# Flamingo gated block: tokens stationary in the first product, the product transposed on TensorE, and a new order within the step

## What is computed

```
def xattn(h, token_ids, W):
    expert = min(clip(token_ids, 0, 24999) // 6250, 3)
    g = silu(einsum('bsd,fd->bsf', h, W[e])); u = einsum('bsd,fd->bsf', h, W[e])
    y = einsum('bsf,df->bsd', g * u, W[e])            # taken where expert == e
def ffn(x, Wr, br, Wd, bd, Wu, bu):
    gates = softmax(x @ Wr + br + bonus); w = top 2 of 8, normalized
    h = relu(einsum('btd,edr->betr', x, Wd) + bd); eo = h @ Wu + bu
    return sum over e of w[e] * eo[e]
x = x + tanh(g_xattn) * xattn(layernorm(x), tokens, ctx)
x = x + tanh(g_ffn) * ffn(layernorm(x), ...)
```

## Time and profile before

| | before |
|---|---|
| median of three runs | 239.81 us (238.13 to 240.24) |
| the profiled execution | 238.26 us, span 236.5 us |
| mean granted TensorE clock | 0.938 |
| PE busy | 181.9 us, 77% of the span |
| VectorE busy | 140.0 us, 59% |
| ScalarE busy | 121.8 us, 51% |
| POOL busy | 115.6 us, 49% |
| the chain that ended last | POOL 28%, issue 26%, PE 15%, VectorE 14%, its queue 9% |

### The profile page before, as it was taken

The page is one execution under the profiler, slowest core; times in us unless marked ns, Lnnn a source line. Parts: engine busy times, 40 slices in busy tenths (PEclk is TensorE's granted clock), DMA queues, the critical chain, the costliest instruction groups (busy, mean ns, idle before and its releaser), DMA issues.

```text
span 236.5 us, 5853 instructions
## 1 busy us (share of the span) xinstructions
PE 181.9 (77%) x1558; PEld 119.6 (51%) x1559; DVE 140.0 (59%) x452; ACT 121.8 (51%) x254; POOL 115.6 (49%) x261
## 2 busy tenths in 40 slices
PE   1767978789999887888698787889869985835550
PEld 1746953546666555464455645556456562413310
DVE  5778837576766665757656565545755745444421
ACT  2875893983476645628365473654734535401200
POOL 3678443536155837455473534534446446422421
PEclk9999997999999999999999999999999999597655
DMA  5947751323139343331333313343134032120111
GB/s 178 355 110 259 160 124 39 94 47 84 55 87 136 78 99 98 88 91 44 89 85 95 89 44 91 70 110 89 44 89 99 34 89 49 41 81 8 44 44 44
DMA packets 43028, 21.62 MB, mean 91 GB/s; under 512 B 38632, under 2 KB 38760, under 8 KB 43008
## 3 DMA queue, kind: packets, MB, share of 16 engines
q1 hardware_dynamic: 40448, 12.99, 23.5%
q0 software_dynamic: 2560, 8.39, 11.1%
HBM read 9.06 MB, written 4.19 MB: 56 GB/s over the span
## 4 chain that ended last, share of the span: by engine, by line
POOL 28%; issue 26%; PE 15%; DVE 14%; DVEq 9%; ACT 4%; ACTq 2%; DMA 1%; POOLq 1%
POOL rs L501 6%; POOL xs L483 4%; DVEq L1229 4%; DVEq L1230 3%; POOL neg_mean L567 3%; POOL half_second L540 3%; PE ps_aT L682 3%; POOL mrs L502 3%; POOL ve L500 2%; DVE xs L1236 2%; POOL half_first L538 2%; ACT dev L870 2%; DVE w_rep L1289 2%; DVE w_lo L1096 2%; POOL hot_slot L476 2%
## 5 line engine op out<-in xcount | busy, mean ns | idle before, releaser
L682 PE MATMUL ps_aT<-hT,w_hi 128*128 128x128 f16 x304 | 64.8, 228 | 1.7 <-DVE prod L1212 1.0
L683 PE MATMUL ps_aT<-hT,w_hi 128*128 128x128 f16 x304 | 63.4, 223 | 0.0
L684 PE MATMUL ps_aT<-hT,w_lo 128*128 128x128 f16 x304 | 63.3, 223 | 0.0
L682 PEld LDWEIGHTS ps_aT<-hT,w_hi 128*128 x304 | 30.0, 99 | 15.1 <-issue 4.1
L658 PE MATMUL ps_y<-w_hi,pT_hi 128*128 x76 | 30.3, 399 | 2.4 <-DVE w_lo L1096 1.9
L1236 DVE SCALAR_TENSOR_TENSOR xs<-ps_y,y_t,xs 128x512 f32 x19 | 14.3, 751 | 30.2 <-issue 27.1
L683 PEld LDWEIGHTS ps_aT<-hT,w_hi 128*128 x304 | 30.5, 100 | 1.3
L660 PE MATMUL ps_y<-w_hi,pT_lo 128*128 x76 | 30.3, 399 | 0.0
L684 PEld LDWEIGHTS ps_aT<-hT,w_lo 128*128 x304 | 30.0, 99 | 0.6
L659 PE MATMUL ps_y<-w_lo,pT_hi 128*128 x76 | 30.2, 397 | 0.0
L870 ACT ACTIVATE dev<-xs,neg_mean 128x512 f32<-128x512 f32 (+1 forms) x15 | 10.8, 722 | 30.1 <-POOL neg_mean L567 30.1
(11 more groups left out here) (217 smaller groups left out, 424.8 us busy)
## 6 DMA issues: line engine op xcount, KB each, us to landing
w_nat<-in_ctx_dram SPq DMA_DIRECT2D x4, 1024.0 KB, 7.6
xs<-in_x_dram,rows_of POOLq DMA_INDIRECT x16, 3.6
wd_nat<-in_L_ffn_Wd_dram SPq DMA_DIRECT2D x4, 64.0 KB
wu_nat<-in_L_ffn_Wu_dram SPq DMA_DIRECT2D x1, 256.0 KB
hT<-h_parts SPq DMA_TRANSPOSE x16, 2.7
out_dram<-xs,rows_of POOLq DMA_INDIRECT x16, 2.9
h2T<-h_parts SPq DMA_TRANSPOSE x15, 2.8
b_in<-in_L_ffn_bd_dram SPq DMA_DIRECT2D x1, 64.0 KB
```

The costliest lines, as they stand in the source:

```text
L682: mm(ps_aT[:, n, :], hi, hT[:, q, kc, :], start=(kc == 0), stop=False)
L683: mm(ps_aT[:, n, :], hi, hT[:, q, KC + kc, :], start=False, stop=False)
L684: last = mm(ps_aT[:, n, :], lo, hT[:, q, kc, :], start=False, stop=(kc == KC - 1))
```

## The change

The first product has the tokens stationary (`split_product` into ps_a): 12 matmuls of 512 columns. Its result has tokens in partitions, so the silu and the product work on that layout, and TensorE transposes the fp32 product in four pieces into ps_pT (`transpose_product`); `product_high` and `pT_low` read it from there. `neg_mean` moves from POOL to ScalarE. VectorE compares the indices (`picked`), and `choice` keeps two of its five operations on POOL; the factor that they held goes into the scale of `weighted_high` and `weighted_low`. The small tensors of `hidden` and `weigh` are doubled by the tile's parity, `hidden` is one step later (i-7), the low-rank part too (i-8), and the last tile gets banks of its own, so that the tail runs two tiles side by side. `place` stands at the step's start on VectorE, the load of the tile number on ScalarE too.

```
-            def first_product(k, q, e, blocks):
-
-                for n in blocks:
-                    for kc in range(KC):
-                        cols = slice(n * P, (n + 1) * P)
-                        hi = w_hi[:, bass.ds(e, 1), kc, cols].rearrange("p e n -> p (e n)")
-                        lo = w_lo[:, bass.ds(e, 1), kc, cols].rearrange("p e n -> p (e n)")
-                        mm(ps_aT[:, n, :], hi, hT[:, q, kc, :], start=(kc == 0), stop=False)
-                        mm(ps_aT[:, n, :], hi, hT[:, q, KC + kc, :], start=False, stop=False)
-                        last = mm(ps_aT[:, n, :], lo, hT[:, q, kc, :], start=False, stop=(kc == KC - 1))
-                return last
+            def transpose_product(k):
+
+                pe.wait_ge(prod_done, k + 1)
+                wait_last(pe, pT_lo_done, k)
+                for c in range(KC):
+                    last = tr(ps_pT[:, c, :], prod[:, c * P:(c + 1) * P], ident[:, :])
+                last.then_inc(pT_done, 1)
+
+            def is_last(k):
...
+                if some(T, -5 - LATE, i0):
+                    transpose_weighted(i - 5 - LATE, (i0 - 5 - LATE) % 2)
+                if has_y:
+                    transpose_product(i - 1)
+                if some(T, -4 - LATE, i0):
+                    hidden_product(i - 4 - LATE, (i0 - 4 - LATE) % 2)
                 if has_a:
                     if isinstance(i, int) and i < E:
                         wait_low(pe, i)
@@ -740,20 +772,14 @@
                         pe.wait_ge(hT_lo_done, i + 1)
                     else:
                         landed(pe, s_hT, i, q, ON_PE)
-                    wait_last(pe, prod_done, i)
-                    first_product(i, q, e_now, range(0, KC // 2))
-                if some(T, -4 - LATE, i0):
-                    transpose_weighted(i - 4 - LATE)
-                if has_a:
-                    first_product(i, q, e_now, range(KC // 2, KC)).then_inc(a_done, 1)
+                    split_product(ps_a, hT[:, q, 0:KC, :], hT[:, q, KC:2 * KC, :], e_now)\
+                        .then_inc(a_done, 1)
+                if some(T, -5 - LATE, i0):
+                    low_rank_out(i - 5 - LATE, (i0 - 5 - LATE) % 2)
...
-                act.wait_ge(prod_done, k + 1)
+                act.wait_ge(pT_done, k + 1)
                 wait_last(act, y_done, k)
-                a(pT_hi[:, :, :], prod[:, :, :], ACT.Copy).then_inc(pT_hi_done, 1)
-
-            def weighted_high(k):
+                a(pT_hi[:, :, :], ps_pT[:, :, :], ACT.Copy).then_inc(pT_hi_done, 1)
+
+            def weighted_high(k, q):
 
                 act.wait_ge(wtT_done, k + 1)
-                wait_last(act, o_mm, k)
-                a(wT_hi[:, 0, :], ps_wT[:, 0, :], ACT.Copy)
-                a(wT_hi[:, 1, :], ps_wT[:, 1, :], ACT.Copy, scale=low_rows[:, :]).then_inc(wtT_hi_done, 1)
+                if not (isinstance(k, int) and k < 2):
+                    act.wait_ge(o_mm, k - 1)
+                bank = wT_bank(k)
+                a(wT_hi[:, q, 0, :], bank[:, 0, :], ACT.Copy, scale=half_s[:, :])
+                a(wT_hi[:, q, 1, :], bank[:, 1, :], ACT.Copy, scale=low_half_s[:, :]).then_inc(wtT_hi_done, 1)
+
+            def negative_mean(k):
...
+                act.wait_ge(x1_done, k + LATE + 1)
+                a(neg_mean[:, col(k)], row_sum[:, col(k)], ACT.Copy, scale=-1.0 / D).then_inc(neg_mean_done, 1)
...
+                has_h, has_2 = some(NP, 3, i0), some(T - 1, -2 - LATE, i0)
+                if has_h:
+                    tile = tile_of(i + 3)
+                if some(T, -5 - LATE, i0):
+                    weighted_high(i - 5 - LATE, (i0 - 5 - LATE) % 2)
                 if some(NP, -1, i0):
                     product_high(i - 1)
-                if some(T, -4 - LATE, i0):
-                    weighted_high(i - 4 - LATE)
                 if meanwhile:
                     meanwhile()
-                if some(T - 1, -2 - LATE, i0):
+                if has_h:
+                    normalize(i + 3, (i0 + 3) % 2, tile, not some(T, 3, i0))
+                if has_2:
+                    negative_mean(i - 2 - LATE)
                     deviations(i - 2 - LATE)
-                if some(NP, 3, i0) and not early:
-                    normalize(i + 3, (i0 + 3) % 2, not some(T, 3, i0))
-                if i0 == 1:
-                    normalize(3, 1, False)
-                if some(NP, 0, i0):
-                    act.wait_ge(a_done, i + 1)
-                    a(silu[:, :, :], ps_aT[:, :, :], ACT.Silu, scale=inv_t[:, col(i)]).then_inc(silu_done, 1)
-                if early and 0 <= i + 1 < ON_PE:
-                    hT_high(i + 1)
-                if early and 0 <= i + 2 < ON_PE:
-                    normalize(i + 2, (i + 2) % 2, False)
-                if i0 == 1:
-                    normalize_high(3, 1)
-                    normalize(4, 0, False)
-                    normalize_high(4, 0)
-                if some(T - 1, -2 - LATE, i0):
+                if some(T, -4 - LATE, i0):
+                    tanh_gap(i - 4 - LATE, (i0 - 4 - LATE) % 2)
+                silu_of(i, i0 % 2)
+                if has_2:
                     normalize2(i - 2 - LATE)
                     normalize2_high(i - 2 - LATE, (i0 - 2 - LATE) % 2)
-                if some(T, -3 - LATE, i0):
-                    tanh_gap(i - 3 - LATE)
-                if some(NP, 3, i0) and not early:
+                if has_h:
                     normalize_high(i + 3, (i0 + 3) % 2)
...
+            for i in range(-4, NP):
                 if i == 0:
                     y_factors(1, 0, 2)
                 if 0 < i + 1 < E:
                     low_part(i + 1)
                 if i == 2:
                     y_factors(2, 2, NP)
+                if i > -4:
+                    gather(i + 4 + AHEAD)
+                if 0 <= i - 4 - LATE:
+                    choice(i - 4 - LATE)
+                if 0 <= i - 2 - LATE:
+                    rstd_of_rows(i - 2 - LATE)
                 if 0 <= i + 4 < T:
                     pool.wait_ge(aggr1, i + 5)
                     rstd(0, mv1[:, 0:1], -1.0, mv1[:, 1:2], 1.0, i + 4, rstd1)
+                if 0 <= i - 5 - LATE:
+                    rows_out(i - 5 - LATE)
                 if i == -4:
                     pairs_tiles()
-                gather(i + 4 + AHEAD)
-                k = i - 3 - LATE
-                if 0 <= k < T:
-                    choice(k)
-                k = i - 4 - LATE
-                if 0 <= k < T:
-                    rows_out(k)
+                    gather(AHEAD)
+            rstd_of_rows(T - 2)
+            choice(T - 4)
+            rows_out(T - 5)
+            pool.wait_ge(aggr2, 1)
+            rstd(1, mv2[:, 0:1], -1.0, mv2[:, 1:2], 1.0, T - 1, rstd2)
+            choice(T - 3)
+            rows_out(T - 4)
+            choice(T - 2)
+            choice(T - 1)
+            rows_out(T - 3)
+            rows_out(T - 2)
+            rows_out(T - 1)
...
-                pool.wait_ge(arg_done, k + 1)
-                then(g.tensor_copy(arg8f[:, :], arg8[:, :]))
-                if k:
-                    pool.wait_ge(w8_done, k)
-                g.tensor_scalar(half_first[:, :], slot_no[:, 0:EF], arg8f[:, 0:1], half_s[:, :],
-                                  ALU.is_equal, ALU.mult)
-                then(g.tensor_scalar(half_second[:, :], slot_no[:, 0:EF], arg8f[:, 1:2], half_s[:, :],
-                                       ALU.is_equal, ALU.mult))
-                g.tensor_tensor(half_sum[:, :], half_first[:, :], half_second[:, :], ALU.add)
-                g.tensor_tensor(half_dif[:, :], half_first[:, :], half_second[:, :],
-                                  ALU.subtract).then_inc(mix_done, 1)
+                q = k % 2
+                pool.wait_ge(picked_done, k + 1)
+                if k > 1:
+                    pool.wait_ge(w8_done, k - 1)
+                g.tensor_tensor(both[:, q, :], picked[:, q, 0, :], picked[:, q, 1, :], ALU.add)
+                g.tensor_tensor(differ[:, q, :], picked[:, q, 0, :], picked[:, q, 1, :],
+                                ALU.subtract).then_inc(mix_done, 1)
...
+                v.tensor_tensor(picked[:, q, :, :], expert_no[:, :].unsqueeze(1).to_broadcast([P, 2, EF]),
+                                arg8[:, q, 0:2].bitcast(i32).unsqueeze(2).to_broadcast([P, 2, EF]),
+                                ALU.is_equal).then_inc(picked_done, 1)
...
+            def step(i, i0):
+
+                where = place(i - 1)
+                if some(T, -5 - LATE, i0):
+                    weighted_low(i - 5 - LATE, (i0 - 5 - LATE) % 2)
                 if some(T, -4 - LATE, i0):
-                    add_low_rank(i - 4 - LATE)
+                    hidden(i - 4 - LATE, (i0 - 4 - LATE) % 2)
+                pT_low(i - 1)
+                if some(T, 4, i0):
+                    statistics1(i + 4)
+                if some(T, -5 - LATE, i0):
+                    add_low_rank(i - 5 - LATE)
+                if some(T, -4 - LATE, i0):
```

(40 more changed lines are left out.)

302 lines of the change are left out of this document (174 added, 128 removed).

## The result

The kernel after takes 197.39 us (median of four runs, 196.13 to 198.33), the kernel before 239.25 us on the same chip: ratio 0.825, 95% interval 0.818 to 0.831. The profiled execution took 196.88 us.

A forecast was written before the change was run, and what follows sets the result against it. The prediction took a loop through several engines to bound the kernel, 8.1 us per step after the change; savings of 28.1 us from 238.26 gave 210.2, and 0.65% for the median gave 211.5 us, range 204 to 223.

The forecast's parts named there:

- What bounds the kernel before: Steady steps: no engine is full; a loop through ScalarE, VectorE and POOL, `add_y` to `add_y`, sets 9.9 us.
- The new loop: New steady step: from `add_y` through `hidden`, choice, second norm, ScalarE's high part and low parts to `add_y`, 8.1 us.
- if they begin as soon behind `add_y`: VectorE's two loads start 0.11 us behind the issue of `add_y` and run beside its 0.75 us; `wT_lo` starts at 1.8.
- PE at most 7.7: PE's products and transposes cost at most 7.7 us per new step, 0.9 less than before, and fit within the loop.
- So 8.1 us per step, set by the loop: Steady steps: the loop through the engines sets 8.1 us; the other two bounds, VectorE and PE, are 7.8 and 7.7.
- rival 2: Steady steps: loop shorter, PE bounds at 7.5 us if hidden matmuls are quicker than 81 ns; 204.5 us; chance 0.10.
- PE pauses there as before, at a clock that falls: Step to the last `add_y`: low-rank add waits for a product behind the second one; 9.9 against 10.2, 0.3 us saved.
- The tail: Last `add_y` to last output row: two tiles side by side, low-rank products at low clock; 16.0 against 19.2, 3.2 saved.
- Rival 1: VectorE's first load waits for `add_y`'s accumulator read; `wT_lo` 0.7 us later in twelve steps, 220 us; chance 0.17.
- Rivals 3 and 4: Steady steps: gain lost in POOL and ScalarE hand-offs, 235 us (0.08); TensorE clock at 1.2 GHz, slower (0.05).
- Rival 4: TensorE at 1.2 GHz: some 13.5 us per step, slower from six such steps, 275 us with all twelve; chance 0.05.
- The longer loop by a held choice: POOL's choice held until VectorE's `pT_lo` ends: loop 0.6 us longer, 7 us over twelve steps; left out, smaller chance.

The follow-up runs named there:

- Run 15: Kernel before with ScalarE's silu ahead of the square of the deviations: 231.59 us, ratio 0.966.
- run 10: Kernel before, in its own order, with only the first product's new form (12 matmuls of 512 columns, four transposes of the product): 230.66 us, ratio 0.965.
- runs 1 to 3: Kernel after with, in turn, the norm ahead of the choice on POOL, VectorE's loads directly ahead of `add_y`, and both: 197.53, 195.82, 195.99 us.
- run 7: Kernel after with VectorE doing `pT_lo` twice, once into a spare tile: 204.49 us, ratio 0.852, step 7.83 us.
- run 11: Kernel after in its new order, with the old first product (48 matmuls of 128 columns, weights stationary, no product transposes): 200.17 us, ratio 0.842.
- run 14: Kernel after with the old first product, the hidden product half a step earlier on PE and VectorE's loads directly ahead of `add_y`: 206.51 us, ratio 0.857.
- run 2: Kernel after with VectorE's two loads back directly ahead of `add_y`: 195.82 us, ratio 0.820, step 7.44 us.
- run 1: Kernel after with the second norm ahead of the choice on POOL: 197.53 us, ratio 0.822, step 7.50 us.
- run 4: Kernel after with the second product's four matmuls by `w_lo` left out (that part of the result missing): 187.42 us, ratio 0.784, step 7.00 us.

## Why the prediction was wrong, point by point

**What bounds the kernel before: right in the main.** Run 15 shows the loop. That PE has no part in it was too strong: run 10 shortens the first product and gives 8 us, though PE was never full. The silu in the loop waits for that product; how much of the 8 us comes from there, the runs do not separate.

**The new loop: right but for one term.** From the start of one `add_y`, forecast and measured: `wT_lo` 1.8 and 1.14; `hidden` 2.15 and 1.54; `picked` done 3.3 and 2.65; choice done 3.8 and 3.10; `h` 5.2 and 4.56; high part done 6.8 and 6.13; `h2_low` 6.9 and 6.16; `add_y` 8.1 and 7.37. The difference arises at `wT_lo` and stays at 0.6 to 0.7. The term that failed is "if they begin as soon behind `add_y`". The first load of the kernel after in this step (duration in ns, least, median, most; first and last start):

```profile
L1304 DVEq TENSOR_LOAD <-pair_tile_i x1: 327/327/327, 115.1 to 115.1; - x1
```

It began 0.2 us ahead of `add_y` (115.29), while `h_low` ran, and the two were done at 116.4, after 1.3 us and not 1.67 (the first of the two took 0.33 us, before 0.57). A load does not wait until the operation ahead of it starts. The start varies: in the step before it came 0.4 us ahead of `add_y` (107.5), in a later one 0.1 behind it (137.6), and the bare part goes up to 0.7.

**PE at most 7.7: 7.41.** The hidden product was charged 81 ns per matmul, 1.0 us; its matmuls start 59 ns apart, 0.71. The bound "at most" was right, and using it as the value was not: that is where 0.3 us of every PE step came from.

**"So 8.1 us per step, set by the loop": wrong, the step that failed.** Loop and PE come to 7.37 and 7.41, and runs 1 to 3 show that PE holds the step: the loop can be made half a microsecond and more shorter for nothing. That is rival 2, which had 0.10. VectorE's own work, 7.8 in the forecast with statistics, is about 6.9 (run 7). Rival 2 named the condition (matmuls quicker than 81 ns) and gave 204.5; it was priced with a gain in twelve steps only, and left the first steps, the last one and the tail as forecast. The sign that the prediction gave for PE as the bound, `add_y` waiting for the second product, is absent from 108 to 152 us: VectorE waits for PE one product earlier, 4.2 us in five steps at the low-rank add, and is on time for `add_y`.

**The sum**, forecast and measured in the two profiled executions:

| stretch | forecast us | measured us |
|---|---|---|
| up to the sixth `add_y` | 80.7 | 78.95 |
| ten steps | 81.0 | 73.40 |
| two steps | 15.4 | 14.69 |
| the last step | 9.9 | 7.64 |
| to the last output add | 16.0 | 13.4 |
| to the end of the span | 5.3 | 6.0 |
| outside the span | 1.8 | 2.8 |

- Up to the sixth `add_y`: its last step was summed as 7.2 with 1.6 us of bare loads. They were hidden here too, VectorE waited 0.5 for ScalarE instead, and the step took 6.11.
- The last step: of "PE pauses there as before, at a clock that falls" the pause came (1.26 us ahead of the second product, for `pT_lo`) and the fall of the clock did not. From 170 to 174.8 us the granted clock was 1.00 (before, in 200 to 210 us, 0.66); the second product took 2.60.
- The tail: the low clock was to make the last low-rank products 3.0 us; they took 1.4 from `wT_lo` to the last add, since PE had the full clock there: their matmuls start 0.22 us apart. The hidden products just before ran at 0.11 us a matmul, twice their time in the steady steps. Statistics to low part took 6.1, as forecast.
- Rival 1 (loads find no cover, 0.17) is refuted by the rows. The Trainium skill, page "TensorE: Matmul & The Clock Gate", in its table gives VectorE a strict queue 8 deep; it speaks for a load running beside queued operations, and the row on the first load agrees.
- Rivals 3 and 4: the hand-offs cost what the rows of before gave, and the clock stayed at 1.00 through all steady steps. The longer loop by a held choice was rightly left out of the sum: `differ` took its 0.20 us at 110.82, in the middle of `pT_lo`; the two POOL operations of the choice took 0.20 in the median, once 0.32. Rival 4 is mis-summed: twice 0.22 us for 28 matmuls adds 6.1 to 7.7, 13.8 us and not 13.5, so that five such steps and not six would make it slower than before.
- Chances and range: direction right, range too high at its low end. The errors of the steps and of the clock have one sign, because each term took the dearer of two bounds (loads bare, matmuls at 81 ns, clock falling), which is no middle.

## What to carry to other kernels

When a loop and an engine come out within some tenths of a microsecond, compute the engine's sum from the start-to-start distances of each form in the trace, not from an upper bound; which of the two holds the step is then told by shortening the loop alone, not by reading waits. Register loads cost what is left when the work queued ahead of them is spent: put operations that are ready ahead of them (1.2 us of them were enough here to leave 0.28 us or nothing bare), in whatever place. Look at the loads of every engine: PE has a pair too. And an order can be worth ten times the cheaper matmul form: here 38 us against 4 on top of it.

## What the runs showed of the hardware

- A matmul of 128 columns, with weights loaded for each, starts 56 ns behind the last in some stretches and about 80 ns in others (run 11: the first 42 and the rest of one product; run 14: all 48 at the slow pace in one step); in the kernel before the 81 ns were read as its price.
- The two register loads on VectorE can begin ahead of an operation that has not started (115.1 against 115.29). Behind two low parts, 1.2 us, and directly ahead of `add_y`, 0.28 us of 1.3 or nothing stays bare (run 2); behind `add_y`, 0.4 to 0.7 (kernel after) and up to 0.83 (run 1); behind 0.29 us of work 1.77.
- PE's own two register loads take 1.4 us per step. With a second product of 1.7 us they leave up to 0.38 us of PE bare (run 4), and the first products with 128 columns are the slower the later these loads end (2.84 to 2.94 us against 3.54 to 3.59 in run 11).
